# The copies of the turned attention weights of a wide tile, made by one ACT instruction over two PSUM banks

## The reference

```
k = concatenate([mem_k, k]); v = concatenate([mem_v, v])        # 4 memory keys ahead of 1024
dots = einsum('bhid,bhjd->bhij', l2norm(q), l2norm(k)) * 10     # 16 heads of 64
dots = einsum('hg,bgij->bhij', W_pre_th, dots)                  # heads mixed
dots = where(causal, -max, dots)
vk   = top_k(dots, 64)[0][..., -1:]
attn = softmax(where(dots < vk, -max, dots))
attn = einsum('hg,bgij->bhij', W_post_th, attn)                 # heads mixed again
out  = einsum('bhij,bhjd->bhid', attn, v)
```

## Time and profile before

| | us |
|---|---|
| median of 3 runs | 4131.17 |
| lowest, highest | 4124.45, 4132.26 |
| the profiled execution, its own time | 4126.99 |
| its span, first to last instruction | 4125.2 |
| PE matmul, busy | 3379.2 (82%) |
| DVE, busy | 2947.7 (71%) |
| ACT, busy | 2531.9 (61%) |
| POOL, busy | 2038.0 (49%) |

### The profile page before, as it was taken

How to read it: one execution, slowest core, us unless ns; L and a number is a source line. 1 busy time by engine, 2 the same in 40 slices (tenths; PEclk the granted TensorE clock), 3 DMA queues, 4 the chain that set the end, 5 groups by cost and what they waited for, 6 DMA issues and landing times. The chain is left out here.

```text
span 4125.2 us, 73074 instructions
## 1 busy us (share of the span) xinstructions
PE 3379.2 (82%) x22948; PEld 2149.6 (52%) x22948; DVE 2947.7 (71%) x6613; ACT 2531.9 (61%) x5828; POOL 2038.0 (49%) x5809
## 2 busy tenths in 40 slices
PE   4999999994678898888888868899888888887766
PEld 3444444441455556655556645555665555665444
DVE  3888777774578888678888867888866888873333
ACT  1334334432478889678888737888976888882111
POOL 0112112223576667577666647766757766671111
PEclk8999999997689999889999968999997999998887
DMA  2122222212455654345555225555434555521000
GB/s 101 67 92 92 82 87 82 82 74 100 121 151 159 174 162 114 85 142 159 167 168 138 72 81 143 168 164 167 120 84 130 166 163 170 136 54 40 20 20 25
DMA packets 362895, 466.35 MB, mean 113 GB/s; under 512 B 30132, under 2 KB 294708, under 8 KB 362168
## 3 DMA queue, kind: packets, MB, share of 16 engines
q1 hardware_dynamic: 362424, 461.02, 38.0%
HBM read 226.57 MB, written 234.36 MB: 112 GB/s over the span
## 5 line engine op out<-in xcount | busy, mean ns | idle before, releaser
L1386 ACT ACTIVATE junk<-D,nt 128x76 int8<-128x76 f32 (+62 forms) x1440 | 1070.6, 746 | 178.6 <-POOL nt L1471 142.1
L1299 PE MATMUL banks<-kr,E 128*128 128x128 f32 (+1 forms) x4672 | 736.9, 308 | 192.8 <-issue 94.6
L1299 PEld LDWEIGHTS banks<-kr,E 128*128 128x128 f32 (+1 forms) x4672 | 630.5, 210 | 302.7 <-issue 279.1
L1272 PE MATMUL banks<-Sg,kpre 128*128 128x109 f32 (+51 forms) x1568 | 649.0, 514 | 18.2 <-DVE D L1598 9.1
L1258 PE MATMUL banks<-kT,qT 64*128 64x343 f32 (+11 forms) x896 | 401.0, 530 | 213.6 <-DVE Sn L1587 161.6
L1409 ACT ACTIVATE AT<-banks 128x512 f32<-128x512 f32 (+3 forms) x768 | 345.3, 478 | 328.2 <-PE banks L1317 164.6
L1677 DVE SCALAR_TENSOR_TENSOR E<-D,vk,E 128x12 f32<-128x12 f32 (+56 forms) x512 | 378.4, 757 | 211.8 <-DVE vk L1633 131.8
L1587 DVE COPY Sn<-banks 128x686 f32<-128x686 f32 (+7 forms) x448 | 376.6, 841 | 142.2 <-PE banks L1259 132.1
L1613 DVE SCALAR_TENSOR_TENSOR W<-SG,sgn,W 128x76 f32<-128x76 int8 (+14 forms) x480 | 412.7, 899 | 84.6 <-POOL W L1487 82.5
L933 DVE RECIPROCAL a_ri<-a_rr 128x512 f32<-128x512 f32 x128 | 429.2, 3353 | 4.4
L1317 PE MATMUL banks<-AT,V 128*64 128x64 f32 x9216 | 367.1, 232 | 61.5 <-issue 46.8
(11 more groups left out here) (188 smaller groups left out, 5600.1 us busy)
## 6 DMA issues: line engine op xcount, KB each, us to landing
score_scratch<-Sn SPq DMA_DIRECT2D x96, 343.0 KB, 3.2
q_scratch<-a_qn SPq DMA_DIRECT2D x32, 512.0 KB, 2.8
v_scratch<-a_vo SPq DMA_DIRECT2D x32, 512.0 KB, 3.6
k_scratch<-a_qn SPq DMA_DIRECT2D x32, 512.0 KB, 2.8
gate_scratch<-a_gs SPq DMA_DIRECT2D x32, 512.0 KB, 2.7
kT<-k_scratch SPq DMA_DIRECT2D x32, 512.0 KB, 4.7
qT<-q_scratch SPq DMA_DIRECT2D x32, 512.0 KB, 6.1
gateT<-gate_scratch SPq DMA_DIRECT2D x32, 512.0 KB, 11.9
```

The lines of the kernel that those rows point to most:

```text
L1272: out = nc.tensor.matmul(bank[:, 0:c], kpre[:].rearrange("p h r -> p (h r)"), Sg[:, g % 3, c0:c1], start=True, stop=not diagonal)
L1299: out = nc.tensor.matmul(ps[5 + i % 2][0:rows, c % 4 * P:(c % 4 + 1) * P], E[:, g % 4, c * P:c * P + rows], kr[:, g % 4, :], start=True, s ...
L1386: nc.scalar.activation(out, D[:, e, 1:1 + n], ACT.Sign, bias=nt[:, r, e:e + 1], scale=-1.0, accum_out=cnt[:, r, e:e + 1]).then_inc(s[f"cnt ...
```

## The change

Two tables are made. `TURN` gives each group its bank, 0 or 1: the groups of a tile that has more than one go to bank 5, 6, 5; a tile with one group takes the bank that the group before it did not take. `BEFORE` gives for each group the last earlier one in the same bank, and PE waits for that one in place of group i - 2. On ACT, `turned` waits for both groups of a wide tile, copies all its ib + 1 full chunks with one instruction that reads on from bank 5 into bank 6, and raises `at` by two. The short chunk is copied after it, and where it is a third group it is waited for separately. Tiles with one group keep one instruction as before.

```diff
--- before.py
+++ after.py
@@ -1076,6 +1076,12 @@
 
         return LAST[m]
 
+    TURN = []
+    for g in range(NT):
+        groups = len(turn_groups(g))
+        TURN += [j % 2 for j in range(groups)] if groups > 1 else [1 - TURN[-1] if TURN else 0]
+    BEFORE = [max([j for j in range(max(0, i - 4), i) if TURN[j] == v], default=-1) for i, v in enumerate(TURN)]
+
     def searched(p):
 
         return 0 <= p < S and 2 * p % (IB * TPB) >= FIRST
@@ -1292,11 +1298,11 @@
                 ib = g // TPB % IB
                 for j, chunks in enumerate(turn_groups(g)):
                     i = PC[g] + j
-                    if i >= 2:
-                        pe.wait_ge(s["at"], i - 1)
+                    if BEFORE[i] >= 0:
+                        pe.wait_ge(s["at"], BEFORE[i] + 1)
                     for c in chunks:
                         rows = P if c <= ib else MEM
-                        out = nc.tensor.matmul(ps[5 + i % 2][0:rows, c % 4 * P:(c % 4 + 1) * P],
+                        out = nc.tensor.matmul(ps[5 + TURN[i]][0:rows, c % 4 * P:(c % 4 + 1) * P],
                                                E[:, g % 4, c * P:c * P + rows], kr[:, g % 4, :], start=True, stop=True)
                     out.then_inc(s["post"], 1)
 
@@ -1400,20 +1406,24 @@
                 ib, t, hb = g // TPB % IB, g % 8, g // 8
                 if t == 0 and hb >= 1:
                     act.wait_ge(s["av"], hb)
-                for j, chunks in enumerate(turn_groups(g)):
-                    i = PC[g] + j
-                    act.wait_ge(s["post"], i + 1)
-                    bank, full = ps[5 + i % 2], [c for c in chunks if c <= ib]
-                    if full:
-                        c0, c = full[0], len(full)
-                        out = nc.scalar.activation(AT[:, c0:c0 + c, :, t * R8:(t + 1) * R8],
-                                                   bank[:, 0:c * P].rearrange("p (c h r) -> p c h r", h=H, r=R8),
-                                                   ACT.Copy)
-                    if len(full) < len(chunks):
-                        c = (ib + 1) % 4
-                        out = nc.scalar.activation(ATt[:], bank[0:MEM, c * P:(c + 1) * P].rearrange(
-                            "p (h r) -> p h r", h=H), ACT.Copy)
-                    out.then_inc(s["at"], 1)
+                rows = slice(t * R8, (t + 1) * R8)
+                memory = ib + 1 in turn_groups(g)[-1]
+                tail = ps[5 + TURN[PC[g + 1] - 1]][0:MEM, (ib + 1) % 4 * P:((ib + 1) % 4 + 1) * P].rearrange(
+                    "p (h r) -> p h r", h=H)
+                first = min(PC[g] + 2, PC[g + 1])
+                act.wait_ge(s["post"], first)
+                if ib + 1 > 4:
+                    turns = banks[:, 5:7, :].rearrange("p b (c h r) -> p (b c) h r", h=H, r=R8)
+                    out = nc.scalar.activation(AT[:, 0:ib + 1, :, rows], turns[:, 0:ib + 1], ACT.Copy)
+                else:
+                    turns = ps[5 + TURN[PC[g]]][:, 0:(ib + 1) * P].rearrange("p (c h r) -> p c h r", h=H, r=R8)
+                    out = nc.scalar.activation(AT[:, 0:ib + 1, :, rows], turns, ACT.Copy)
+                if memory and first == PC[g + 1]:
+                    out = nc.scalar.activation(ATt[:], tail, ACT.Copy)
+                out.then_inc(s["at"], first - PC[g])
+                if first < PC[g + 1]:
+                    act.wait_ge(s["post"], PC[g + 1])
+                    nc.scalar.activation(ATt[:], tail, ACT.Copy).then_inc(s["at"], 1)
 
             act.wait_ge(s["sig"], 1)
             nc.scalar.activation(sigma[:], wvar[:], ACT.Sqrt, scale=QK_SCALE * QK_SCALE / DH).then_inc(s["sig"], 1)
```

## The result

| | us |
|---|---|
| before, median of 7 runs on the same chip as the changed kernel | 4127.94 (4124.45 to 4132.26) |
| changed, median of 7 runs | 4150.43 (4134.74 to 4154.58) |
| ratio, 95% interval | 1.0045 (1.0027 to 1.0062) |
| profiled execution of the changed kernel, its span | 4140.04, 4138.2 |
| span before, for comparison | 4125.2 |

The changed kernel is slower by 0.45%, 18.6 us with 11 to 26 as the ends of the interval (ratio less 1, times 4128). The forecast was 9.4 us, range 4127 to 4155; the median lies in the range, the sign is right and the size was set at half. The two profiled spans differ by 13.0 us only: the seven runs of the changed kernel lie within 20 us, and the profiled one is the second lowest of them.

A forecast was written before the change was run, and what follows sets the result against it. No engine alone bounds wide blocks; PE, ACT and DVE hand tiles around in a ring. Drain 5.3, batch ends 3.3, rest of ib 7 0.8, ib 4 to 6 0: 9.4 us on 4131.17, so 4140.6, range 4127 to 4155.

The forecast's parts named there:

- The saved instruction: On ACT, 256 wide tiles each lose one instruction worth 0.05 us: 12.8 us of ACT's time at most.
- The hand-over in the drain: Drain of batch 3: PE and ACT take turns, 3.22 us a tile against 1.91; 0.5 + 3.9 + 0.9 = 5.3 us.
- The batch ends: Ends of batches 0 to 2: the short chunk waits for the whole copy, `values` 1.1 us late each, 3.3 us.
- The rest of ib 7 and ib 4 to 6: Rest of ib 7: net 0.2 us a batch, 0.8; ib 4 to 6: 0, with ends -9.6 and +14.4 us.
- 2 us a batch: The forecast would be wrong if ib 4 to 6 grew or shrank by more than 2 us a batch.
- within 1 us: Durations of the wide blocks, apart from the drain and batch ends, stay within 1 us of before.
- a fall of PE's clock: Drain: PE's pauses might drop it from 2.4 to 1.2 GHz, turning a tile then costing up to twice 1.9 us.
- The savings pass: Rival, 18%: ACT sets the pace in all wide blocks, 12.8 us come off the forecast, 4127.8 us.
- the delays pass on in ib 4 to 6, and PE's idle time lets its clock fall more often: Rival, 22%: late copies have no slack in ib 4 to 6, 14.4 us more than the forecast, 4155 us.
- Extra cost of a read over two banks: Rival, 5%: one ACT instruction reading two banks costs extra or saves nothing; 0.05 us a tile more, partly passing, 4146 us.

The follow-up runs named there:

- hold_two: Changed kernel with its waits, but two copy instructions behind the one wait, `at` raised by two after the second; ratio to the kernel before 1.0041.
- mid_only: Kernel before with one copy only for the 192 wide tiles of ib 4 to 6, bank by bank in ib 7; 4125.95 us, ratio 0.9986.
- head_only: Kernel before with one copy only for t = 0 to 8 of ib 7 (36 tiles), bank by bank elsewhere; 4130.29 us, ratio 0.9996.
- drain_only: Kernel before with one copy only for t = 9 to 15 of ib 7 in batch 3 (seven tiles); 4135.74 us, ratio 1.0021.
- late_only: Kernel before with one copy only for 120 tiles of ib 4 to 7 picked by its trace as free of cost; 4129.17 us, ratio 0.9991.
- filled: Changed kernel with five extra matmuls in PE's pauses before ib 7's short chunks and tiles 11 to 15 of batch 3; ratio to the kernel before 1.0043.
- tails_only: Kernel before with one copy only for t = 9 to 15 of ib 7 in every batch (28 tiles); 4151.74 us, ratio 1.0048.

## Why the prediction was right, and where it was short

- **The saved instruction.** Forecast 0.05 us each on ACT, nothing at the end. The rows of after: 0.92 us from the start of a 1024-column copy to the next instruction (3712.15, 3713.07), where two copies of 512 took 0.49 each, so 0.06 with the rounding. Over the whole traces the median distance of starts is 904 ns for 1024 columns and 477 for 512, so 0.05. Right, and hold_two shows no part of it in the time; a part of it in ib 4 to 6 is left open by mid_only. The Trainium skill, "ScalarE: Activation LUTs", gives 186 ns plus 0.833 ns a column and an overlap of about 93 ns back to back (section "What ACT_TABLE_LOAD costs"), which makes 93 ns of fixed cost as an estimate from that page. The rows have about half of that, and the measurement decides.
- **The hand-over in the drain.** Forecast 3.22 us a tile, measured 3.29. The start of the row of four (from t = 12) came 0.8 late and not 0.5, the three hand-overs cost 4.1 and not 3.9, the short chunk 1.1 and not 0.9: 6.0 against 5.3 until `values` begins. The walk tile by tile holds.
- **The batch ends.** Forecast 1.1 us each, measured 1.1 where the clock was not in play (2.89 to 4.00 us until `values`, 8.21 to 9.33 for the turn).
- **The rest of ib 7 and ib 4 to 6.** Forecast 0.8 and 0. Both lie within the intervals of head_only and mid_only, which are wide enough for some us either way. In head_only's profile the first came to 1.4: the delay of 0.4 us stayed in three batches, and the 0.2 that four savings were to win back did not come. ib 4 to 6 differ by +1.2, +1.0, -0.4 and -0.6 us in the profile of the change, within the 2 us a batch that the prediction allowed. Its "within 1 us" for the other wide blocks failed: the first half of ib 7 took 2.1 us more in two batches, by the clock.
- **What was short is the clock.** The prediction named a fall of PE's clock as a risk of the pauses in the drain, left it "to the range", and had it nowhere in the sum; it also looked for it in the turning matmuls. It came behind them, in `values`. Measured between the first turnings of tiles in the profile of the change, the first halves of ib 7 are 3.5 us longer than before (2.1, 2.1, 0.4 and -1.1 in the four batches), forecast 0.8. From t = 8 on it is 14.0 (0.4, 7.2, 0.4, and 6.0 until the last `values` begins), forecast 8.6. Together that is 17.5 against 9.4, near the 18.6 of the medians. Four pieces of it are matmuls at the low clock: 1.9 in each of two first halves, 1.8 for the last tile of batch 1 and 2.8 in the `values` behind it. Without these 8.4 the 17.5 would be 9.1. That this meets the 9.4 so closely is partly luck: low clock at other places, in either profile, is not counted. The 1.8 is not shown to be the change's doing, as drain_only has it too. The rest of the span goes the other way, narrow blocks -3.9, ib 4 to 6 +1.2, last stage -1.8, so the two spans differ by 13.0 only.
- **The rivals.** "The savings pass", in full, fell by hold_two. Of "the delays pass on in ib 4 to 6, and PE's idle time lets its clock fall more often" the first half fell by mid_only, and the second half is what the rows show; its time of 4155 had no price for the clock in it, so that it lies nearer to the result than the forecast's is luck. "Extra cost of a read over two banks" fell by the 1.02 us copy.

What stays open: how much of the difference between 9.4 and 18.6 us in the medians is PE's clock, and how much is scatter. In the narrow blocks, whose instructions are the same in all kernels, the profiles differ from before by -3.9 us (the change) to +15.6 (late_only), added up between the same turnings, so one profile cannot settle it. That the pauses are what makes the clock fall in `values` rests on the counts (three of four profiles at the turn of batch 1 and three of six in the drain, none of the others); filled, which was to test it, did not show it in the time.

## What to carry to other kernels

A pair of buffers between two engines is worth as much as the halves that are released one at a time: joining two copies into one instruction turns the pair into a single buffer that both engines must wait for in full. Price such a merge by the gap between starts (here 0.05 us), not by the duration of the instruction (0.60), and set against it one whole copy for each place where the producer follows itself closely. Those places are seldom the steady blocks; look at the drain and the seams, where 28 of 256 tiles alone lost as much as the whole change. And test the parts together as well as apart: here two parts that cost nothing measurable alone brought a lower clock in the first half block of ib 7 once both were in.

## What the runs showed of the hardware

ACT read across two PSUM banks with one instruction at the price of its columns: 1.02 us for 1024, where two copies of 512 took 1.08 together.

PE pausing 1.2 to 1.3 us before each 2 us of work kept the full clock in the drain in the profile of the change (all turnings 2.02 us), but in three other profiles of the same stretch (tails_only, hold_two, drain_only) the granted clock then dropped to 1.2 GHz inside the `values` that followed; the rows of tails_only above show three such groups. Kernels with the same instructions at a place show the drop in one profile and not in another.

The level of the clock differs also where the instructions are those of before: in batch 1 of drain_only the last tile took 4.01 us for 18 matmuls, 2.36 before. Single executions of one kernel scatter by more than the change is worth: the 29 to 35 runs of before in the larger sessions lie within 29 to 33 us.
